# Phase one of a graph network layer: fp32 rows turned once per tile and multiplied in fp32, in place of three bf16 parts

## The chip, the cores and the metric

The kernel runs on one core of a Trainium2 chip. The metric is the device time of one execution in microseconds, the median of the runs given. The engines are TensorE (PE, with its weight loads as PEld), VectorE (DVE), ScalarE (ACT), GpSimd (POOL) and SyncE (SP, which here only issues transfers).

## The reference

Two graph layers over 100,000 nodes of 32 features and 25,000 edges that are sorted by dst. Only the first is touched:

```python
h = maximum(layernorm(x), 0)
x = x + L0(h, src, dst, attr3, attr10, weight)     # phase one
x = x + L1(maximum(layernorm(x), 0), src, dst)     # attention, phase two

# L0: xs = scalars (8) of both ends, xv = vectors (8 x 3) of both ends, 16 each
h = sqrt(2) * relu(emb @ W1 / sqrt(10))                    # (E, 16)
w = (h @ W2 / 4).reshape(E, 7, 16, 8)                      # weights of each edge
s_out = PW_S * (xs . wa_s + (xv . y1) . wb_s / sqrt(3))    # g_out alike
v_out = PW_V * (xs y1 . wc + xv . wd + (xv W3J y2) . we)
out   = segment_sum([tanh(s_out), tanh(g_out) * v_out] * norm, dst)
```

The kernel multiplies each edge's 80 numbers by W2 for each of the 16 hidden units first, and then weights the 16 results by the edge's h and adds them.

## The kernel before

Each of 128 partitions holds T = 196 consecutive edges, and a tile is one edge of each partition. Seven tiles (GA) make a group, and there are NG = 28 groups. GpSimd gathers the rows of x at src and at dst, one indirect transfer for each tile and side, paced by semaphores in `paced(t)`.

Phase one is software-pipelined over the groups, with the order of each engine's instructions written out by hand in a function `group(k, b)` of each engine. For group g+1, VectorE's `normalize` writes `hrow`: for each tile 5 units of 16 fp32 columns (the scalars of both ends, three components of the vectors, and the vectors' product with the edge's direction). ScalarE's `first_parts` and `second_parts` and VectorE's `first_rest` and `third_part` split these into three bf16 parts, stacked as 6 slots of 16 columns for each unit. TensorE's `turn_units` transposes the 35 units of a group in five chunks of seven, through two PSUM banks (turnA, turnB), and ScalarE's `turned` copies each chunk to SBUF.

`product(g, b, t)` multiplies a tile's turned stacks (K = 96) by W2: two matmuls of 384 columns for scalars and gates and three of 128 for the vectors, into one of two buffers of PSUM, `tens`. A product waits until the tile before the last has been read from its buffer. VectorE's `multiply` weights six of the seven tiles by the hidden values (L1408), and ScalarE's `multiply` weights tile 3 in 16 instructions (L809). TensorE then adds the 16 terms with an identity matrix: `sum_first` for tiles 0 to 2 after VectorE's `halve`, `sum_rest` for tiles 3 to 6. VectorE's `outputs` makes `vmix` from these sums, ScalarE's `gates` takes tanh, and VectorE's `messages` scans the running sums.

TensorE's order in a group is: products 0 and 1, `turn_emb`, chunks 2 and 3, `sum_first(g-1)`, chunk 4, product 2, `sum_rest(g-1)`, product 3, the hidden product, products 4 and 5, chunks 0 and 1 of g+1, product 6. ScalarE's is: the first and second parts, `gates(g-1)`, `multiply` (tile 3), squares of g+2, the hidden values, chunks 0 and 1, deviation, chunks 2 to 4 with `keep_run` and `flags` between. Into this are woven the layer norms of all nodes in 28 slices of "dense" rows, some of them beside the edge groups in `SLICE1`:

```python
SLICE1 = {g: d for d, g in enumerate(g for g in range(-1, NG)
          if g not in (2, 5, 8, 11, 14, 16, 17, 20, 22, 24, 25, 27))}
```

With g in SLICE1, VectorE takes row sums and centres in group g, then the variance, and scales and adds in group g+1; each of these five passes is over 124x928 elements.

Before the loop, W2 is loaded, scaled, split into three bf16 parts on VectorE, and copied by 18 transfers of SP's queue (L601, L602) into the stacks `w_s` and `w_v`. Behind phase one come a search for the sums of the source nodes, and phase two, which is of the same shape as phase one, in fp32.

Of the kernel before, what the change touches and what calls it, by code (L numbers as in the profile page):

```python
# [5 lines left out]
F32 = mybir.dt.float32  # L6
# [22 lines left out]
def build_gnn(nc, x, src, dst, attr10, attr3, weight, W1, W2, Wq, Wk, Wv, Wout, out):  # L29
# [8 lines left out]
    SC = 4 * MOUT  # L38
# [18 lines left out]
    assert 0 < TAIL <= T and NG % 2 == 0 and GA % 2 == 1 and NCH % 2 == 1 and T % GA == 0 and 0 < DLAST < DR and DREM <= DP and HEADS == 4  # L57
    assert N <= 4 * 25600 and UNITS * GA == CH * NCH

# [41 lines left out]
    with ctx:  # L101
# [9 lines left out]
        def part(area, at, *dims, parts=P):  # L111
# [4 lines left out]
                if len(dims) > 1 else v  # L116
# [34 lines left out]
        turned_area = sb("stack_turned", [P, UNITS * GA, P], BF16)  # L151
        at = 0
        stack = part(agg, at, SLOTS * NR * ROW // 2).bitcast(BF16).rearrange("p (n s c) -> p n s c", s=SLOTS, c=VU)
        at += SLOTS * NR * ROW // 2
        stackT = [part(agg, at, UNITS * GA * P // 2, parts=KU).bitcast(BF16).rearrange("c (u e) -> c u e", e=P),
                  turned_area[0:KU]]
        at += UNITS * GA * P // 2
# [6 lines left out]
        rest = part(agg, at, UNITS * GA, VU)  # L164
        at += NR * ROW
# [3 lines left out]
        hflat = hrow.rearrange("p t u c -> p (t u) c")  # L169
# [68 lines left out]
        numer = part(turned_area[:, :, :].rearrange("p u e -> p (u e)").bitcast(F32), 0, 2, HEADS * F1, GA + 1)  # L238
# [28 lines left out]
        identb = sb("identb", [P, P], BF16)  # L267
        eps = sb("eps", [P, 1])
        wscale = sb("wscale", [P, 1])
# [52 lines left out]
        w2s = part(h1d_area, at, HID, OG, parts=SC)  # L322
        at += HID * OG
# [6 lines left out]
        w2s_rest = part(h1d_area, at, HID, OG, parts=SC)  # L330
        at += HID * OG
        w2v_rest = part(h1d_area, at, HID, MOUT, parts=VU)
        at += HID * MOUT
        w2s_part = part(h1d_area, at, 3 * HID * OG // 2, parts=SC).bitcast(BF16).rearrange(
            "p (a j o) -> p a j o", a=3, o=OG)
        at += 3 * HID * OG // 2
        w2v_part = part(h1d_area, at, 3 * HID * MOUT // 2, parts=VU).bitcast(BF16).rearrange(
            "p (a j o) -> p a j o", a=3, o=MOUT)
        at += 3 * HID * MOUT // 2
# [42 lines left out]
        s_w2p = sem("w2_parts_ready")  # L382
        s_w2 = sem("w2_stacks_loaded")
# [29 lines left out]
        s_hi = sem("first_parts_ready")  # L413
        s_r1 = sem("first_rests_ready")
        s_mid = sem("second_parts_ready")
        s_lo = sem("stacks_ready")
        s_turn = sem("units_turned")
        s_turned = sem("turned_units_on_sbuf")
# [106 lines left out]
        N_STACKS = 3 * SLOTS  # L525
# [3 lines left out]
        def _(sp):  # L529
# [107 lines left out]
        def _(pool):  # L637
# [6 lines left out]
            pool.wait_ge(s_id, 1)  # L644
            nc.gpsimd.tensor_copy(identb[:], ident[:]).then_inc(s_id, 1)

            def paced(t):

                if t == 10:
                    pool.wait_ge(s_gsb, 1)  # L650
                elif t == 11:
                    pool.wait_ge(s_w2p, 1)
                elif t == 12:
                    pool.wait_ge(s_cen, 1)
                elif t == 13:
                    pool.wait_ge(s_h, 1)
                elif t == 14:
                    pool.wait_ge(s_hi, 1)
                elif t == 15:
                    pool.wait_ge(s_lo, 1)  # L660
                elif 15 < t < 20:
                    pool.wait_ge(s_turned, t - 15)
                elif t >= 20:
                    pool.wait_ge(s_tens, max(t - AHEAD + 1, (3 * (t - 19) + 3) // 4))
# [53 lines left out]
        def _(act):  # L718
# [11 lines left out]
            for rows, plan in ((slice(0, VU), (WA_S, WA_G, WC)), (slice(VU, SC), (WB_S, WB_G, WE))):  # L730
                for col, which in enumerate(plan):
                    load(w2s[rows, :, col * MOUT:(col + 1) * MOUT], w2_rows[which])
# [69 lines left out]

# [28 lines left out]
            first_parts(0)  # L831
            second_parts(0)
# [3 lines left out]
            turned(0, 0, range(2))  # L836
            dense_square(0)
            square(1)
            turned(0, 0, range(2, NCH))
# [3 lines left out]
            def group(k, b):  # L843
# [23 lines left out]
                if next1:  # L867
                    turned(g + 1, 1 - b, range(2, 3))
                if past(g, 0):
                    keep_run(g - 1, 1 - b)  # L870
                if next1:
                    turned(g + 1, 1 - b, range(3, 4))
                flags(g, b)
                if next1:
                    turned(g + 1, 1 - b, range(4, NCH))

# [131 lines left out]
        def _(pe):  # L1008
            pe.wait_ge(s_id, 2)
# [23 lines left out]
            pe.wait_ge(s_feat, 16 * 9)  # L1033
            pe.wait_ge(s_w2, 16 * N_STACKS)

# [13 lines left out]
            def turn_units(n, b, chunks):  # L1049
                pe.wait_ge(s_lo, n + 1)  # L1050
                for c in chunks:
                    if past(n, 0) or c > 1:
                        pe.wait_ge(s_turned, n * NCH + (c - 1))
                    bank = turn[(b + c) % 2][0:KU, :].bitcast(BF16)
                    for i in range(CH):
                        mm = nc.tensor.transpose(bank[:, i * P:(i + 1) * P],  # L1056
                                                 stack[:, c * CH + i].rearrange("p s c -> p (s c)"), identb[:])
                    mm.then_inc(s_turn, 1)

            def product(g, b, t):  # L1060
                pe.wait_ge(s_turned, g * NCH + ((UNITS * t + UNITS - 1) // CH + 1))
# [34 lines left out]
            def group(k, b):  # L1096
# [24 lines left out]
            turn_units(0, 0, range(2))  # L1121
# [120 lines left out]
        def _(dve):  # L1242
# [8 lines left out]
            v.memset(dprev_i, 0).then_inc(s_padf, 1)  # L1251
            v.memset(w1bd[:], 0.0)
# [18 lines left out]
            v.memset(wscale[0:SC], 1.5 ** 0.5 * PW_V)  # L1271
            v.drain()
            v.memset(wscale[0:VU], PW_V)
# [66 lines left out]
            v.tensor_scalar(w2s[:, :, 0:2 * MOUT], w2s[:, :, 0:2 * MOUT], PW_S, None, ALU.mult)  # L1340
            v.tensor_scalar(w2s[:, :, 2 * MOUT:], w2s[:, :, 2 * MOUT:], wscale[0:SC, 0:1], None, ALU.mult)
# [3 lines left out]
            v.drain()  # L1345
            for which in range(3):
                for whole, left, parts in ((w2s, w2s_rest, w2s_part), (w2v, w2v_rest, w2v_part)):
# [525 lines left out]
```

## Time and profile before

| | us |
|---|---|
| median of 3 timed runs (1193.73 to 1196.26) | 1195.46 |
| span of the profiled execution | 1442.6 |
| profiled span over the median | 247.1 |
| PE busy, share of the span | 856.9, 59% |
| DVE busy | 982.3, 68% |
| ACT busy | 842.4, 58% |
| POOL busy | 794.9, 55% |
| mean granted TensorE clock | 0.76 |

The profile is of one execution, whose own time is its span, from the first to the last instruction; what lies around the span is not recorded. Busy time counts an engine's own work; waits do not count. The granted clock is a share of full speed: 1.00 is 2.4 GHz and 0.50 is 1.2 GHz. Phase one lies between about 45 and 785 us of the span, the search between 785 and 1100, and phase two after it. In the chain of waits, each piece is the work or the wait that the next piece had to wait for.

### The profile page before, as it was taken

The page shows a single profiled execution, that of the slowest core. Times are in us where ns is not written, and L with a number is a line of the kernel's source. Part 1 is how long each engine was busy: PE and PEld are TensorE (multiplying, and loading weights), DVE is VectorE, ACT ScalarE, POOL GpSimd, SP SyncE. Part 2 cuts the span into 40 slices and gives each one's busy share as a digit, 9 for nine tenths or more (in the row PEclk, how much of TensorE's full clock was granted, in tenths as well). Part 3 has the DMA queues.
Part 4 walks back from the last instruction along what each step waited for, and adds up shares of the span by engine and source line. Part 5 has one row for each costly group of instructions (what it writes and reads, how often), then busy time and mean ns, then how long its engine had stood idle before and what let it go on. Part 6 is the DMA issues. An engine that isn't in the chain of part 4 may idle for free.

```text
span 1442.6 us, 16871 instructions
## 1 busy us (share of the span) xinstructions
PE 856.9 (59%) x5248; PEld 690.5 (48%) x5248; DVE 982.3 (68%) x1799; ACT 842.4 (58%) x2035; POOL 794.9 (55%) x796
## 2 busy tenths in 40 slices
PE   0256777677776877777874221323135777777773
PEld 0245665566565756666773110211123565555552
DVE  4566686777776667566664635865336999998984
ACT  0346665666766575666754333746244887787871
POOL 5664565466554665455004455775752665656664
PEclk9988688878777777767786555555557999999986
DMA  4121021111111102111014213432300000000000
GB/s 114 19 56 35 16 50 22 43 28 46 58 41 29 37 10 62 34 36 23 16 52 163 76 37 84 115 109 76 88 20 5 10 9 9 9 9 9 9 9 7
DMA packets 40669, 60.52 MB, mean 42 GB/s; under 512 B 17361, under 2 KB 31077, under 8 KB 40324
## 3 DMA queue, kind: packets, MB, share of 16 engines
q1 hardware_dynamic: 12216, 46.86, 10.2%
q0 software_dynamic: 25184, 12.32, 5.4%
q8 instruction: 43, 0.70, 0.2%
q10 hardware_dynamic: 3180, 0.26, 0.2%
q14 instruction: 46, 0.38, 0.1%
HBM read 40.33 MB, written 19.37 MB: 41 GB/s over the span
## 4 chain that ended last, share of the span: by engine, by line
PE 21%; ACT 21%; DVE 20%; another core or an unknown queue 16%; DVEq 10%; issue 8%; SPq 1%; DMA 1%; POOL 0%; POOLq 0%
PE sums L1080 9%; ACT h1d_or_products L809 5%; DVEq L1764 4%; PE tens L1070 3%; ACT below L900 3%; PE turnB L1056 3%; PE turnA L1056 2%; ACT stack_turned L800 2%; DVEq L1705 2%; DVE run L1753 2%; ACT agg_or_stacks L800 2%; DVE tens L1725 2%; PE tens L1074 2%; DVE dcen L1748 1%
## 5 line engine op out<-in xcount | busy, mean ns | idle before, releaser
L674 POOL DMA_INDIRECT x_rows<-in_x,src_index x196 | 196.1, 1001 | 228.9 <-PE tens L1074 146.3
L701 POOL DMA_INDIRECT out_dram<-agg_or_stacks,scatter_index x196 | 193.6, 988 | 144.6 <-ACT agg_or_stacks L974 90.4
L694 POOL DMA_INDIRECT agg_or_stacks<-run_sums,sum_row_index x196 | 203.1, 1036 | 112.3 <-issue 57.9
L674 POOL DMA_INDIRECT x_rows<-in_x,dst_index x196 | 197.2, 1006 | 64.9 <-issue 64.9
L1408 DVE TENSOR_TENSOR h1d_or_products<-tens,hid 128x768 f32<-128x768 f32 x168 | 158.8, 952 | 64.8 <-PE tens L1074 42.8
L1080 PE MATMUL sums<-h1d_or_products,ident 128*128 128x192 f32 x896 | 174.4, 356 | 4.8 <-issue 4.2
L1080 PEld LDWEIGHTS sums<-h1d_or_products,ident 128*128 128x128 f32 x896 | 164.9, 212 | 11.3 <-issue 11.1
L1143 PE MATMUL sums<-one_column,halves_or_steps 128*128 128x1 f16 x112 | 22.1, 197 | 176.6 <-DVE halves_or_steps L1564 62.0
L967 ACT ACTIVATE features_or_rows<-stack_turned,is_last 128x132 f32<-128x132 f32 x196 | 85.9, 520 | 39.3 <-DVE stack_turned L1735 39.3
L1143 PEld LDWEIGHTS sums<-one_column,halves_or_steps 128*128 128x128 f16 x112 | 14.1, 126 | 197.7 <-ACT below L900 73.2
L1070 PE MATMUL tens<-w_scalar_stacks,agg_or_stacks 96*128 96x384 bf16 x196 | 66.5, 432 | 65.9 <-ACT h1d_or_products L809 41.4
L1070 PE MATMUL tens<-w_scalar_stacks,stack_turned 96*128 96x384 bf16 x196 | 66.6, 433 | 62.2 <-ACT h1d_or_products L809 48.8
L900 ACT ACTIVATE below<-sums,bias_of_src 128x196 bf16<-128x196 f32 x112 | 46.5, 420 | 83.6 <-remote 55.2
L800 ACT COPY stack_turned<-turnB 96x896 bf16<-96x896 bf16 x42 | 37.9, 902 | 97.1 <-remote 68.4
L809 ACT ACTIVATE h1d_or_products<-tens,hid 128x48 f32<-128x48 f32 x448 | 88.8, 358 | 0.1
L1080 PE MATMUL sums<-halves_or_steps,ident 128*128 128x144 f32 x448 | 83.1, 351 | 3.4 <-issue 3.1
L1391 DVE TENSOR_TENSOR agg_or_stacks<-agg_or_stacks 128x560 f32<-128x560 f32 x28 | 20.8, 741 | 91.0 <-ACT agg_or_stacks L791 91.0
L800 ACT COPY agg_or_stacks<-turnA 96x896 bf16<-96x896 bf16 x42 | 38.0, 904 | 73.3 <-remote 47.5
L1080 PEld LDWEIGHTS sums<-halves_or_steps,ident 128*128 128x128 f32 x448 | 78.6, 250 | 3.2 <-issue 3.2
L1212 PE MATMUL turnB<-features_or_rows,ident 128*128 128x132 f32 x448 | 60.2, 290 | 31.1 <-ACT features_or_rows L967 24.5
L1056 PE MATMUL turnB<-identb,agg_or_stacks 128*96 128x128 bf16 x490 | 59.9, 289 | 24.0 <-ACT stack_turned L800 20.6
L1212 PEld LDWEIGHTS turnB<-features_or_rows,ident 128*128 128x128 f32 x448 | 55.3, 197 | 38.1 <-ACT features_or_rows L967 30.1
(308 smaller groups left out, 2536.5 us busy)
## 6 DMA issues: line engine op xcount, KB each, us to landing
src_everywhere<-src_by_columns SPq DMA_DIRECT2D x14, 896.0 KB
xin<-in_x SPq DMA_DIRECT2D x27, 449.5 KB
out_dram<-xin SPq DMA_DIRECT2D x27, 449.5 KB
x_rows<-in_x,src_index POOLq DMA_INDIRECT x196
x_rows<-in_x,dst_index POOLq DMA_INDIRECT x196
run<-run_sums SPq DMA_DIRECT2D x1, 3136.0 KB
agg_or_stacks<-run_sums,sum_row_index POOLq DMA_INDIRECT x196
out_dram<-agg_or_stacks,scatter_index POOLq DMA_INDIRECT x196
```

Source lines behind the costliest of these rows:

```text
L674: nc.gpsimd.indirect_dma_start(xs[:, t, side, :], None, x, bass.IndirectOffsetOnAxis(ap=idx[:, t:t + 1], axis=0)).then_inc(s_gath[g % LEAD ...
L694: nc.gpsimd.indirect_dma_start(aggr[:, t, :], None, rs, bass.IndirectOffsetOnAxis(ap=ridx[:, t:t + 1], axis=0)).then_inc(s_rsg[t // GA], 16)
L701: nc.gpsimd.indirect_dma_start(out, bass.IndirectOffsetOnAxis(ap=sidx[:, t:t + 1], axis=0), aggr[:, t, :], None, bounds_check=N - 1, oob_i ...
L800: nc.scalar.copy(stackT[b][:, c * CH:(c + 1) * CH, :].rearrange("c u e -> c (u e)"), turn[(b + c) % 2][0:KU, :].bitcast(BF16)[:, 0:CH * P] ...
L809: last = nc.scalar.activation(prod[:, 2 * TACT:2 * TACT + 2, j, :], bank[:, :, j * OG:(j + 1) * OG], ACT.Copy, scale=hid[:, b, TACT, j:j + 1])
L900: last = nc.scalar.activation(below[:, t % 4], bank[:, j * T:(j + 1) * T], ACT.Sigmoid, bias=of[:, t:t + 1], scale=256.0, accum_out=to[:, ...
L967: last = nc.scalar.activation(head_rows[:, t, :], numer[:, b, :, 1 + t], ACT.Copy, scale=last_of_first[:, g * GA + t:g * GA + t + 1])
L1056: mm = nc.tensor.transpose(bank[:, i * P:(i + 1) * P], stack[:, c * CH + i].rearrange("p s c -> p (s c)"), identb[:])
L1070: nc.tensor.matmul(bank[:, 0:HID * OG], stackT[b][:, UNITS * t + u, :], w_s[:, i].rearrange("c j o -> c (j o)"), start=(i == 0), stop=(i = ...
L1080: mm = nc.tensor.matmul(sums[:, a * OUTS:b * OUTS].rearrange("p (c o) -> p c o", o=OG), ident[:], terms[:, :, j, :], start=(j == 0), stop= ...
L1212: nc.tensor.matmul(head_sum, ident[:], head_rows[:, t, :], start=(t == 0), stop=(t == GA))
L1408: v.tensor_tensor(prod[:, 2 * t:2 * t + 2], tens[(b + t) % 2][:, :].rearrange("p (a c) -> p a c", a=2)[:, :, 0:HID * OG].rearrange("p a (j ...
```

## The change

The split into bf16 parts goes. `turn_units` turns each tile's 80 fp32 columns of `hrow` at once, in two halves of 4 and 3 tiles (`TURNS`), a whole group ahead, and ScalarE copies the two halves (512 and 384 columns of 80 partitions). A product is two fp32 matmuls with K = 80 and 384 columns each; `w_v` has its columns laid out so that one matmul serves the three components, with zeros where a unit has no weight. The buffers of both turned groups lie in `turned_area`. W2 stays fp32, and 3 transfers in place of 18 copy it. `normalize` waits until the rows before it have been turned. `paced` waits on other semaphores for tiles 14 to 19.

```diff
-    SLOTS = 6
     UNITS = 5
-    KU = SLOTS * VU
+    KU = UNITS * VU
-    CH = 7
-    NCH = UNITS * GA // CH
+    TURNS = ((0, 4), (4, GA))
...
-        w_s = sb("w2_scalar_stacks", [KU, 2, HID, OG], BF16)
-        w_v = sb("w2_vector_stack", [KU, HID, MOUT], BF16)
+        w_s = sb("w2_of_scalars", [KU, HID, OG])
+        w_v = sb("w2_of_vectors", [KU, HID, OG])
...
-            for place, which in enumerate((0, 0, 1, 1, 2, 0)):
-                rows = slice(place * VU, (place + 1) * VU)
-                for u in range(2):
-                    sp.dma_start(w_s[rows, u, :, :], w2s_part[u * VU:(u + 1) * VU, which]).then_inc(s_w2, 16)
-                sp.dma_start(w_v[rows, :, :], w2v_part[:, which]).then_inc(s_w2, 16)
+            for k in range(3):
+                sp.dma_start(w_v[(k + 1) * VU:(k + 2) * VU, :, k * MOUT:(k + 1) * MOUT], w2v).then_inc(s_w2, 16)
...
# ScalarE
-            def first_parts(n):
-                act.wait_ge(s_h, n + 1)
-                nc.scalar.copy(stack[:, :, 0:SLOTS:2, :], spread(hflat, 2, [P, UNITS * GA, 3, VU])).then_inc(s_hi, 1)
-
-            def second_parts(n):
-                act.wait_ge(s_r1, n + 1)
-                nc.scalar.copy(stack[:, :, 1:4:2, :], spread(rest, 2, [P, UNITS * GA, 2, VU])).then_inc(s_mid, 1)
-
-            def turned(n, b, chunks):
-                for c in chunks:
-                    act.wait_ge(s_turn, n * NCH + (c + 1))
-                    nc.scalar.copy(stackT[b][:, c * CH:(c + 1) * CH, :].rearrange("c u e -> c (u e)"),
-                                   turn[(b + c) % 2][0:KU, :].bitcast(BF16)[:, 0:CH * P]).then_inc(s_turned, 1)
+            def turned(n, b, half):
+                of = slice(TURNS[half][0] * P, TURNS[half][1] * P)
+                act.wait_ge(s_turn, n * 2 + (half + 1))
+                nc.scalar.copy(stackT[b][:, of], turn[half][0:KU, 0:of.stop - of.start]).then_inc(s_turned, 1)
...
# ScalarE, group(k, b)
                 if next1:
-                    first_parts(g + 1)
                     take_emb(g + 1)
-                    second_parts(g + 1)
...
                 if next1:
                     hidden(g + 1, 1 - b)
-                    turned(g + 1, 1 - b, range(2))
+                    turned(g + 1, 1 - b, 0)
...
                 flags(g, b)
                 if next1:
-                    turned(g + 1, 1 - b, range(4, NCH))
+                    turned(g + 1, 1 - b, 1)
...
# TensorE
+            def turn_units(n, half):
+                pe.wait_ge(s_h, n + 1)
+                if past(n, 0):
+                    pe.wait_ge(s_turned, n * 2 - 1 + half)
+                first, end = TURNS[half]
+                for t in range(first, end):
+                    mm = nc.tensor.transpose(turn[half][0:KU, (t - first) * P:(t - first + 1) * P],
+                                             hrow[:, t].rearrange("p u c -> p (u c)"), ident[:])
+                mm.then_inc(s_turn, 1)
...
             def product(g, b, t):
...
-                for i, u in enumerate((0, UNITS - 1)):
-                    nc.tensor.matmul(bank[:, 0:HID * OG], stackT[b][:, UNITS * t + u, :],
-                                     w_s[:, i].rearrange("c j o -> c (j o)"), start=(i == 0), stop=(i == 1))
-                vec = bank[:, 512:512 + HID * OG].rearrange("p (j o) -> p j o", o=OG)
-                for k in range(3):
-                    mm = nc.tensor.matmul(vec[:, :, k * MOUT:(k + 1) * MOUT], stackT[b][:, UNITS * t + 1 + k, :], w_v[:],
-                                          start=True, stop=True)
-                mm.then_inc(s_tens, 1)
+                rows = stackT[b][:, t * P:(t + 1) * P]
+                nc.tensor.matmul(bank[:, 0:HID * OG], rows, w_s[:].rearrange("c j o -> c (j o)"), start=True, stop=True)
+                nc.tensor.matmul(bank[:, 512:512 + HID * OG], rows, w_v[:].rearrange("c j o -> c (j o)"), start=True,
+                                 stop=True).then_inc(s_tens, 1)
...
# TensorE, group(k, b)
                 if more:
                     turn_emb(g + 1)
-                turn_units(g, b, range(2, 4))
                 if past(g, 0):
                     sum_first(g - 1)
-                turn_units(g, b, range(4, NCH))
                 product(g, b, 2)
...
                 product(g, b, 4)
+                if more:
+                    turn_units(g + 1, 0)
                 product(g, b, 5)
                 if more:
-                    turn_units(g + 1, 1 - b, range(2))
+                    turn_units(g + 1, 1)
                 product(g, b, 6)
...
# VectorE
+            v.memset(w_s[:], 0.0)
+            v.memset(w_v[:], 0.0)
...
             def normalize(n):
                 dve.wait_ge(s_std, n + 1)
+                if past(n, 0):
+                    dve.wait_ge(s_turn, n * 2)
...
-            def first_rest(n):
-                dve.wait_ge(s_hi, n + 1)
-                v.tensor_tensor(rest, hflat, stack[:, :, 0, :], ALU.subtract).then_inc(s_r1, 1)
-
-            def third_part(n):
-                dve.wait_ge(s_mid, n + 1)
-                v.tensor_tensor(stack[:, :, SLOTS - 1, :], rest, stack[:, :, 1, :], ALU.subtract).then_inc(s_lo, 1)
```

On VectorE the calls of `first_rest` and `third_part` in `group` go too, and the three rounds of casts and subtractions of W2.

## Rows read from the trace of the kernel before

**Rows 1.** The page: the span, and the chain's shares by engine.

```profile
span 1442.6 us, 16871 instructions
...
PE 21%; ACT 21%; DVE 20%; another core or an unknown queue 16%; DVEq 10%; issue 8%; SPq 1%; DMA 1%; POOL 0%; POOLq 0%
```

**Rows 2.** The chain's shares by line, 84 to 780 us.

```profile
by line: PE sums L1080 17.9%; another core or an unknown queue 17.2%; ACT h1d_or_products L809 10.7%; PE tens L1070 7.1%; issue 6.2%; PE turnB L1056 5.1%; PE turnA L1056 4.5%; ACT stack_turned L800 4.5%; ACT agg_or_stacks L800 3.6%; PE tens
```

**Rows 3.** Timeline (start, duration, engine, line, operation [idle before, releaser]).

```profile
418.34 0.95 PE L1056 MATMUL turnA<-identb,agg_or_stacks 128*96 128x128 bf16 x7
...
426.13 0.90 ACT L800 COPY agg_or_stacks<-turnA 96x896 bf16<-96x896 bf16 x1 [8.06 <-remote]
```

**Rows 4.** The chain in order of time (start, duration, what), late in phase one.

```profile
699.98 5.27 PE sums L1080 x32
...
706.31 3.18 ACT h1d_or_products L809 x16
...
709.62 0.80 PE tens L1070 x2
...
717.16 2.73 PE sums L1080 x16
...
720.77 5.27 PE sums L1080 x32
...
741.12 5.27 PE sums L1080 x32
```

**Rows 5.** The chain in order of time, the first 104 us.

```profile
34.58 0.35 DVE h1d_or_products L1348
...
38.00 0.60 SPq L601
...
102.26 1.97 PE sums L1080 x5
```

**Rows 6.** Stretches: length; busy PE, PEld, DVE, ACT, POOL; clock, DMA share, GB/s.

```profile
709.60:718.50 8.90, 8.69 (x55) 7.09 (x56) 7.29 (x13) 6.31 (x10) 0.00 (x0) 0.50 0.01 2
718.60:727.00 8.40, 8.40 (x65) 7.94 (x64) 4.82 (x9) 5.36 (x8) 0.00 (x0) 1.00 0.00 0
727.00:747.35 20.35, 16.29 (x122) 14.02 (x120) 13.09 (x20) 12.35 (x30) 0.00 (x0) 0.83 0.08 22
386.00:409.05 23.05, 17.52 (x119) 14.78 (x120) 19.68 (x31) 16.46 (x37) 12.66 (x14) 0.78 0.14 29
1231.00:1295.00 64.00, 47.45 (x258) 37.71 (x257) 58.73 (x119) 50.93 (x120) 38.45 (x40) 1.00 0.04 9
```

**Rows 7.** Timeline of TensorE in phase two.

```profile
1249.42 1.13 PE L1183 MATMUL tens<-gbd,features_or_rows 128*128 128x512 f32 x2 [1.49 <-ACT features_or_rows L947]
1250.38 0.81 PE L1185 MATMUL tens<-gbd,features_or_rows 96*128 96x384 f32 x2
1251.05 0.70 PE L1199 MATMUL tens<-ubd,features_or_rows 128*128 128x256 f32 x2
...
1259.11 0.27 PE L1177 MATMUL turnA<-ident,h1d_or_products 128*96 128x128 f32 x1
1259.22 0.27 PE L1176 MATMUL turnA<-ident,agg_or_stacks 128*128 128x128 f32 x1
```

**Rows 8.** Groups by line and shape (count | busy us, mean ns | idle before).

```profile
L791 ACT CAST agg_or_stacks<-agg_or_stacks 128x1680 bf16<-128x1680 f32 x28 | 44.7, 1595 | 4.8 <-DVE agg_or_stacks L1387 4.8
...
L795 ACT CAST agg_or_stacks<-agg_or_stacks 128x1120 bf16<-128x1120 f32 x28 | 31.5, 1127 | 26.3 <-DVE agg_or_stacks L1391 23.6 <-issue 2.6
...
L800 ACT COPY agg_or_stacks<-turnB 96x896 bf16<-96x896 bf16 x28 | 25.3, 902 | 19.5 <-remote 12.9 <-PE turnA L1056 4.5 <-PE turnB L1056 1.8
...
L1391 DVE TENSOR_TENSOR agg_or_stacks<-agg_or_stacks 128x560 f32<-128x560 f32 x28 | 20.8, 741 | 91.0 <-ACT agg_or_stacks L791 91.0
```

**Rows 9.** The chain in order of time, 386 to 409 us.

```profile
398.44 2.87 another core or an unknown queue
```

**Rows 10.** Timeline of VectorE: group 2's row sums.

```profile
70.76 0.62 DVE L1359 TENSOR_REDUCE stat<-x_rows 128x14 f32<-128x448 f32 x1 [4.26 <-DMA x_rows<-in_x,dst_index]
```

More of the change, by code:

```diff
@@ L56, in build_gnn @@
     DREM = N - DP * RPP
-    assert 0 < TAIL <= T and NG % 2 == 0 and GA % 2 == 1 and NCH % 2 == 1 and T % GA == 0 and 0 < DLAST < DR and DREM <= DP and HEADS == 4
-    assert N <= 4 * 25600 and UNITS * GA == CH * NCH
+    assert 0 < TAIL <= T and NG % 2 == 0 and GA % 2 == 1 and T % GA == 0 and 0 < DLAST < DR and DREM <= DP and HEADS == 4
+    assert N <= 4 * 25600 and all((b - a) * P <= 512 for a, b in TURNS)
     HALF = T // 2
@@ L148, in build_gnn @@
         h1d = part(h1d_area, 0, T, FEAT)
-        turned_area = sb("stack_turned", [P, UNITS * GA, P], BF16)
+        turned_area = sb("stack_turned", [P, 2 * HEADS * F1 * (GA + 1)])
+        assert 2 * GA * P <= 2 * HEADS * F1 * (GA + 1)
+        stackT = [part(turned_area, b * GA * P, GA * P, parts=KU) for b in range(2)]
         at = 0
[L153 to L157, printed above, removed]
         cen = part(agg, at, NR, FEAT)
@@ L237, in build_gnn @@
         assert at <= T * FEAT
-        numer = part(turned_area[:, :, :].rearrange("p u e -> p (u e)").bitcast(F32), 0, 2, HEADS * F1, GA + 1)
+        numer = part(turned_area, 0, 2, HEADS * F1, GA + 1)
         late = sb("halves_or_steps", [P, CT * P // 2 + 4 * T])
@@ L412, in build_gnn @@
         s_h = sem("normalized_rows_ready")
[L413 to L418, printed above, removed]
+        s_turn = sem("stacks_turned")
+        s_turned = sem("turned_stacks_on_sbuf")
         s_tens = sem("tensor_product_ready")
@@ L657, in paced @@
                 elif t == 14:
-                    pool.wait_ge(s_hi, 1)
+                    pool.wait_ge(s_turn, 1)
                 elif t == 15:
-                    pool.wait_ge(s_lo, 1)
-                elif 15 < t < 20:
-                    pool.wait_ge(s_turned, t - 15)
+                    pool.wait_ge(s_turn, 2)
+                elif t == 16:
+                    pool.wait_ge(s_turned, 1)
+                elif t == 17:
+                    pool.wait_ge(s_turned, 2)
+                elif t == 18:
+                    pool.wait_ge(s_hid, 1)
+                elif t == 19:
+                    pool.wait_ge(s_tens, 1)
                 elif t >= 20:
@@ L729, in _ @@
             load(w2e, w2_rows[WE])
-            for rows, plan in ((slice(0, VU), (WA_S, WA_G, WC)), (slice(VU, SC), (WB_S, WB_G, WE))):
+            for rows, plan in ((slice(0, VU), (WA_S, WA_G, WC)), (slice(KU - VU, KU), (WB_S, WB_G, WE))):
                 for col, which in enumerate(plan):
-                    load(w2s[rows, :, col * MOUT:(col + 1) * MOUT], w2_rows[which])
+                    load(w_s[rows, :, col * MOUT:(col + 1) * MOUT], w2_rows[which])
             for t in range(GA):
@@ L835, in _ @@
             hidden(0, 0)
-            turned(0, 0, range(2))
+            turned(0, 0, 0)
+            turned(0, 0, 1)
             dense_square(0)
             square(1)
-            turned(0, 0, range(2, NCH))
             deviation(1)
@@ L1047, in hidden_product @@
                 nc.tensor.matmul(small[:, P:P + GA * HID], embT[:], w1bd[:], start=True, stop=True).then_inc(s_hps, 1)
[L1049 to L1058, printed above, removed]
+            def turn_units(n, half):
[7 more added lines that the diff above has]
+                mm.then_inc(s_turn, 1)
             def product(g, b, t):
-                pe.wait_ge(s_turned, g * NCH + ((UNITS * t + UNITS - 1) // CH + 1))
+                pe.wait_ge(s_turned, g * 2 + (1 if t < TURNS[0][1] else 2))
                 if past(g, 0) or t > 1:
@@ L1120, in _ @@
             hidden_product(0)
-            turn_units(0, 0, range(2))
+            turn_units(0, 0)
+            turn_units(0, 1)
             group(0, 0)
@@ L1339, in _ @@
             dve.wait_ge(s_wl, 16 * N_LOADS)
-            v.tensor_scalar(w2s[:, :, 0:2 * MOUT], w2s[:, :, 0:2 * MOUT], PW_S, None, ALU.mult)
-            v.tensor_scalar(w2s[:, :, 2 * MOUT:], w2s[:, :, 2 * MOUT:], wscale[0:SC, 0:1], None, ALU.mult)
+            for rows, gain in ((slice(0, VU), PW_V), (slice(KU - VU, KU), 1.5 ** 0.5 * PW_V)):
+                v.tensor_scalar(w_s[rows, :, 0:2 * MOUT], w_s[rows, :, 0:2 * MOUT], PW_S, None, ALU.mult)
+                v.tensor_scalar(w_s[rows, :, 2 * MOUT:], w_s[rows, :, 2 * MOUT:], gain, None, ALU.mult)
             v.tensor_scalar(w2d, w2d, PW_V * 3.0 ** -0.5, None, ALU.mult)
@@ L1344, in _ @@
             v.scalar_tensor_tensor(w2v, w2e, -PW_V * 6.0 ** -0.5, w2d, ALU.mult, ALU.add)
-            v.drain()
-            for which in range(3):
-                for whole, left, parts in ((w2s, w2s_rest, w2s_part), (w2v, w2v_rest, w2v_part)):
-                    v.tensor_copy(parts[:, which], whole if which == 0 else left)
-                v.drain()
-                for whole, left, parts in ((w2s, w2s_rest, w2s_part), (w2v, w2v_rest, w2v_part)):
-                    if which < 2:
-                        v.tensor_tensor(left, whole if which == 0 else left, parts[:, which], ALU.subtract)
-                v.drain()
             v.drain().then_inc(s_w2p, 1)
@@ L1465, in _ @@
             normalize(0)
-            first_rest(0)
-            third_part(0)
             dense_sums(0)
@@ L1524, in group @@
                     dense_sums(SLICE1[g])
-                if next1:
-                    first_rest(g + 1)
                 if g in SLICE1:
@@ L1533, in group @@
                 halve(g)
-                if next1:
-                    third_part(g + 1)
                 if past(g, 0):
```

38 lines of the change are left out of this document (5 added, 33 removed).

## The prediction

> **What bounds the kernel now.** I read the page first. Its span is 1442.6 us, 247.1 more than the median of the timed runs, 1195.46, and 16% of its chain, some 236 us, stands under "another core or an unknown queue" on a kernel of one core [rows 1]. The chain of the edge phase alone says where: 17.2% of 696 us, 120 us [rows 2]. The timeline shows what such a piece is. Seven turns into turnA end at 419.3 by TensorE's records, and ScalarE's copy of that bank starts at 426.13 after 8.06 us of idle time put down to "remote" [rows 3]. In the last three groups, when GpSimd has no gathers left, there is no such piece. I take it that these pieces belong to the profiled execution: 1442.6 - 236 = 1206 is within 1% of the median. So I price a group on the undisturbed ones near 700 to 747 us, apply the difference to the median, and predict nothing about the span.
>
> The chain there is one loop [rows 4]. sum_rest (32 records, 5.27 us) runs to 705.25. VectorE then builds vmix, ScalarE takes the gates and works off tile 3 in 16 instructions of 3.18 us together, and TensorE's product 5, whose PSUM buffer tile 3 held, starts at 709.62: a hand-over of 4.37 us. From there the chain is on TensorE until the next sum_rest at 720.77, 11.15 us: product 5, two banks of turns, products 6, 0 and 1, turn_emb, two more banks, sum_first, the fifth bank, product 2. The loop takes 20.79 us; the next one 20.35. Against it: from the first sum_rest at 102.26 [rows 5] to 741.12 lie 26 intervals, 638.9 us; less the 120 us that is 20.0 each.
>
> The stretches [rows 6] add the clock. From 709.6 to 718.5, behind a wait of 3.1 us, TensorE is granted half speed (1.2 GHz) while it is 98% busy; from 718.6 full speed (2.4 GHz). So 8.9 us of the 11.15 run at half. VectorE is busy for 13.1 us in the light group from 727 and for 19.7 in a group with dense rows on both sides (386.0 to 409.05). By SLICE1 six of the 27 are such "double" groups; ten ("single") carry a dense variance ahead of multiply 6 and a scale and add behind it; eleven are "light": two have no dense rows, nine only row sums and a centre, which fit under sum_rest.
>
> **The change, part by part.**
>
> *Products.* Five bf16 matmuls of 1,152 columns become two fp32 matmuls of 384. An fp32 matmul of 96 rows by 384 columns shows as two records, and from its first to the next line's first is 0.67 us at full clock [rows 7]. K=80 for 96 is no reason for another price. So a product takes 1.33 us at full clock and 2.6 at half. Before, at half, product 5 took 0.80 for its first two matmuls, 1.12 with the other three [rows 4].
>
> *Turns.* Thirty-five bf16 turns become seven fp32 turns. Those that follow one another in phase two start 0.11 us apart [rows 7]; at half I take 0.21. Four (0.44) lie before product 5, in the wait for ScalarE, where they cost nothing as long as products 3 and 4 leave 0.44 of it; three lie between products 5 and 6.
>
> *The loop, light group, full clock.* sum_rest 5.27; hand-over 4.37, nothing in it changed. Then five products 6.65, three turns 0.33, turn_emb 0.11, and sum_first 16 records at 144/192 of sum_rest's 0.165, 1.98: 9.07 instead of 11.15. Together 18.7, 2.1 less than 20.8. That needs the full clock between 709.6 and 718.5, and this is my choice in the sum. During the hand-over TensorE now has product 3, the hidden product (0.2), product 4 and four turns: 1.33 + 0.2 + 1.33 + 0.44 = 3.3, which leaves an idle 1.1 in place of 3.1. In phase two TensorE is 74% busy, with waits of 1.49 us before L1183, and is granted 1.00 over 64 us [rows 6, 7]. The new loop would be 94% busy (17.6 of 18.7) with a shorter wait. The Trainium skill (TensorE: Matmul & The Clock Gate, Part 4) says that turns do not count as activity for the clock. By that rule the quiet piece is 1.5 us, the length that phase two bears, so the sum would stay; the trace neither contradicts nor shows the rule.
>
> *Dense rows.* In a single group ScalarE's square and VectorE's variance sum come ahead of multiply 6, and product 1 waits for that: about 0.75 us more in the new loop, a part of which the old one pays too. I take a gain of 1.3. In double groups VectorE decides. It loses 0.74 for first_rest, as much for third_part of the same shape, and its wait for ScalarE's cast, 91.0 us in all and 3.3 per group [rows 8], nearly the whole of the 3.4 that it idles in that group. So it is busy 18.2 us; with 0.9 for drains and gaps and about 2 of waits for the longer products 5, 6 and 1 (an estimate), it gets round in 21. The old double group, 23.05 less an unknown piece of 2.87 [rows 9], takes 20.2. I take a loss of 1.0, for what the piece hid.
>
> *ScalarE.* It loses 1.60 + 1.13 + 5 x 0.90 = 7.2 us per group and gains two copies of 512 and 384 fp32 columns, some 1.1 by the copy of 896 [rows 8]. None of it is on the loop: tile 3 is released by the gates, and the copy that product 0 waits for stands behind ScalarE's squares, where one of 0.6 replaces two of 0.9. Hidden behind products 5 and 6 (2.7 us), so I take nothing; if this cover went, it would cost its 0.6. normalize's new wait, for the turns of the rows that it overwrites, is met before the group begins: nothing.
>
> *Clock in double groups.* There TensorE idles near 3 us (VectorE is late by 2, ScalarE by 1), the length that costs it the clock now [rows 6]. Busy time at half costs half its length: 4.4 for a stretch like today's 8.9, less for a shorter one. I take 2.6, and charge three of six: 8 us. Bounds: 0 and 6 x 4.4 = 26.
>
> *Start.* SP has 3 weight copies to issue for 18, at 0.60 each, and VectorE none of the splits, which fill the 3.4 us from 34.58 to 38.00 [rows 5]; two memsets of 384 columns are new (under 1). TensorE starts some 10 us earlier, but group 2's last gather, for which VectorE waited 4.26 us [rows 10], is issued by GpSimd at 2.5 us a tile. Bounds of the gain 0 and 12; I take 5, near the row of the wait.
>
> *Sum.* 11 x -2.1 - 10 x 1.3 + 6 x 1.0 = -30; clock +8; start -5: -27 from 1195.46, so 1169 us (1168.5). Phase two, the search and the last gathers are untouched. GpSimd needs 17.5 us for 14 gathers (1.0 and a gap of 0.25 each), under 18.7.
>
> **Rivals.**
> - *The clock stays half behind the hand-over* (the other side). Place: products 5, 6, 0, 1. Each microsecond at half costs 0.5. If 8.9 us per group stay at half as now, the light loop is 18.7 + 4.45 = 23.2, 2.4 over the old one: 27 x 2.4 - 5, 1255. With 3.4 us of it in each of 24 groups: 1169 + 24 x 1.7 = 1210. It turns the sign when more than 2 us per group run at half. For it: fp32 work has more to lose. Against it: the 64 us above. Chance 0.20.
> - *VectorE becomes the bound everywhere.* Multiplies 5, 6, 0 and 1 wait for products of 1.5 us with their way to PSUM, while the dense passes pile up behind. Light groups would gain 0.5 to 1, single ones nothing, double ones lose 1.5: 1185 to 1197. For it: 19.7 busy of 23. Against it: light groups with 13.1. Chance 0.17.
> - *More is gained*: the timed group is the 20.8 of the late groups throughout, double ones included (21.5), and no clock is lost. Then double groups lose nothing, single ones gain 1.7: 11 x 2.1 + 17 + 5 = 45, so 1150; with 10 of start 1145. Chance 0.15.
> - *My forecast*: 1158 to 1183. Chance 0.48.
>
> **Range and chances.** 1169, with 1142 to 1212 for 8 in 10: it takes in the third rival, the second and the short drops of the first. This kernel's runs differ by about 0.2%, 2.4 us. Faster by more: my case, the third rival and a third of the second, 0.68; within 0.2%: 0.07; slower: 0.25.
>
> **What would show it.** In undisturbed groups, sum_rest to sum_rest 18.7 to 19.5, granted clock 1.00 in between, product 5's first two matmuls 1.3 us for four records, a wait before it near 1.1. In double groups VectorE's idle time near 3 us and period 21. The copies of the turned stacks at 0.5 to 0.6 us, two per group. Wrong if the granted clock behind the hand-over is 0.5, if VectorE waits for TensorE in light groups, or if the early groups, which the profile disturbs, go otherwise in the timed runs.

## The result and the profile after

The changed kernel takes 1282.52 us (1280.81 to 1294.43, four runs) where the kernel before takes 1195.62 on the same chip: 1.0758 times as long, with a 95% interval of 1.071 to 1.0806. It is slower by some 87 us. The forecast was 1169 with a range of 1142 to 1212, so the sign and the range both missed.

The page of the changed kernel, to be read against [rows 1]. Its own time is 1280.85 us beside a span of 1279.1.

```profile
span 1279.1 us, 14681 instructions
...
PE 948.2 (74%) x4268; PEld 682.9 (53%) x4268; DVE 941.4 (74%) x1735; ACT 675.5 (53%) x1895; POOL 806.8 (63%) x795
...
PEclk9998977787877878979878655555579999999986
...
PE 40%; ACT 20%; DVE 17%; DVEq 9%; DMA 6%; issue 4%; POOL 3%; SPq 0%; POOLq 0%
PE sums L1033 15%; PE tens L1027 11%; PE tens L1028 11%; ACT h1d_or_products L774 7%; ACT features_or_rows L924 6%; DVEq L1697 4%; POOL x_rows L648 3%; DMA out_dram<-xin 3%; DMA xin<-in_x 3%; ACT L913 3%; DVE run L1686 2%; DVE tens L1658 2%; ACT run L915 2%; ACT below L857 1%; PE turnB L1013 1%
```

There is no "another core or unknown queue" in this chain. TensorE heads it, and the granted clock is 7 or 8 tenths in most slices of phase one. Its chain in order of time, one group from hand-over to hand-over (start, duration, what), against [rows 4]. It is a single group; the light one before it, from 397.2 to 421.2 by its gates, takes the same 24.0, for both have their whole chain on TensorE and ScalarE's tile 3:

```profile
420.94 0.66 PE tens L1028 x2
421.60 0.02 issue
421.62 3.17 ACT h1d_or_products L774 x16
424.80 0.14 issue
424.93 0.88 PE tens L1027 x2
425.81 0.88 PE tens L1028 x2
426.70 0.64 PE turnB L1013 x3
427.34 1.28 PE tens L1027 x2
428.62 1.28 PE tens L1028 x2
...
435.02 0.21 PE small L998
435.23 2.56 PE sums L1033 x16
437.79 0.65 PE tens L1027 x2
438.44 0.65 PE tens L1028 x2
439.08 5.20 PE sums L1033 x32
444.29 0.65 PE tens L1027 x2
...
445.59 0.02 issue
```

From one "issue" behind product 3 to the next it is 23.99 us. All of TensorE's work between 426 and 436 takes twice what the same lines take outside: a matmul of 384 columns 1.28 for 0.65, turn_emb 0.21 for 0.11. The stretches of this kernel say why (columns as in [rows 6]):

```profile
402.20:412.40 10.20, 10.20 (x24) 6.10 (x23) 4.76 (x8) 4.02 (x9) 7.63 (x9) 0.50 0.25 60
412.40:426.00 13.60, 12.21 (x65) 9.92 (x65) 10.35 (x19) 5.12 (x21) 6.36 (x6) 1.00 0.06 7
```

For 10.2 us TensorE is busy without a gap and is granted half speed (1.2 GHz); then comes full speed (2.4 GHz). By the starts of the gates' instruction, once per group, 17 of the 27 intervals are 23.7 to 25.8 us, with a granted clock of 0.73 to 0.79. Nine, in which the clock does not fall, are 19.0 to 21.3, and the last one, behind the last group, is 19.5 with a clock of 0.74. The first gate starts at 92.9 and the last at 708.5: 22.8 us per group.

### The profile page after: what moved, and what is told of

The parts are those of the page before. It is cut to its first block, busy times and chain, and to the rows that moved or that the text cites. A ratio compares the mean times of both kernels' runs of the same rounds, so it can differ in the third digit from the quotient of the medians.

```text
span 1279.1 us, 14681 instructions
## 1 busy us (share of the span) xinstructions
PE 948.2 (74%) x4268; PEld 682.9 (53%) x4268; DVE 941.4 (74%) x1735; ACT 675.5 (53%) x1895; POOL 806.8 (63%) x795
## 4 chain that ended last, share of the span: by engine, by line
PE 40%; ACT 20%; DVE 17%; DVEq 9%; DMA 6%; issue 4%; POOL 3%; SPq 0%; POOLq 0%
PE sums L1033 15%; PE tens L1027 11%; PE tens L1028 11%; ACT h1d_or_products L774 7%; ACT features_or_rows L924 6%; DVEq L1697 4%; POOL x_rows L648 3%; DMA out_dram<-xin 3%; DMA xin<-in_x 3%; ACT L913 3%; DVE run L1686 2%; DVE tens L1658 2%; ACT run L915 2%; ACT below L857 1%; PE turnB L1013 1%
## 5 line engine op out<-in xcount | busy, mean ns | idle before, releaser
L648 POOL DMA_INDIRECT x_rows<-in_x,src_index x196 | 208.2, 1062 | 158.8 <-PE tens L1028 113.6
L1027 PE MATMUL tens<-w_of_scalars,stack_turned 80*128 80x384 f32 x392 | 207.1, 617 | 61.4 <-ACT h1d_or_products L774 40.4
L1028 PE MATMUL tens<-w_of_vectors,stack_turned 80*128 80x384 f32 x392 | 206.1, 615 | 0.0
L1033 PEld LDWEIGHTS sums<-h1d_or_products,ident 128*128 128x128 f32 x896 | 147.6, 191 | 7.2
L1033 PE MATMUL sums<-h1d_or_products,ident 128*128 128x192 f32 x896 | 150.6, 327 | 0.0
L786 ACT ACTIVATE gate<-sums 128x112 f32<-128x112 f32 x28 | 7.4, 263 | 246.8 <-DVE vmix L1421 246.8
L1027 PEld LDWEIGHTS tens<-w_of_scalars,stack_turned 80*128 80x128 f32 x392 | 81.9, 237 | 101.0 <-issue 97.5
L1028 PEld LDWEIGHTS tens<-w_of_vectors,stack_turned 80*128 80x128 f32 x392 | 94.0, 240 | 74.7 <-issue 40.3
L1668 DVE TENSOR_TENSOR_SCAN stack_turned<-run,tens 128x1024 f32<-128x1024 f32 x28 | 63.3, 2261 | 0.2 <-issue 0.2
L754 ACT COPY embT<-small 70x128 f32<-70x128 f32 x28 | 7.3, 261 | 99.5 <-PE small L998 99.5
```

The lines of the kernel that those rows point to most:

```text
L648: nc.gpsimd.indirect_dma_start(xs[:, t, side, :], None, x, bass.IndirectOffsetOnAxis(ap=idx[:, t:t + 1], axis=0)).then_inc(s_gath[g % LEAD ...
L1027: nc.tensor.matmul(bank[:, 0:HID * OG], rows, w_s[:].rearrange("c j o -> c (j o)"), start=True, stop=True)
L1028: nc.tensor.matmul(bank[:, 512:512 + HID * OG], rows, w_v[:].rearrange("c j o -> c (j o)"), start=True, stop=True).then_inc(s_tens, 1)
L1033: mm = nc.tensor.matmul(sums[:, a * OUTS:b * OUTS].rearrange("p (c o) -> p c o", o=OG), ident[:], terms[:, :, j, :], start=(j == 0), stop= ...
L1668: v.tensor_tensor_scan(numer[:, b, 0:HF].rearrange("p n t -> p (n t)"), decay[:, b, 0:HF].rearrange("p n t -> p (n t)"), terms.rearrange(" ...
```

## Experiments

The changed kernel has two places where its clock could be helped: the rows that its matmuls fill (80), and the wait before product 5. Each comparison below is with the kernel before on the same chip.

**e1_k128, e2_k96: the products filled up to 128 or 96 rows.** The spare rows of the turned stacks hold zeros, and so do those of the weights, so that the sums are unchanged.

```diff
+        KP = 128                                   # e2: 96
-        stackT = [part(turned_area, b * GA * P, GA * P, parts=KU) for b in range(2)]
+        stackT = [part(turned_area, b * GA * P, GA * P, parts=KP) for b in range(2)]
-        w_s = sb("w2_of_scalars", [KU, HID, OG])
+        w_s = sb("w2_of_scalars", [KP, HID, OG])   # w_v likewise
-                nc.scalar.copy(stackT[b][:, of], turn[half][0:KU, 0:of.stop - of.start]).then_inc(s_turned, 1)
+                nc.scalar.copy(stackT[b][0:KU, of], turn[half][0:KU, 0:of.stop - of.start]).then_inc(s_turned, 1)
+            v.memset(turned_area[0:KP, 0:2 * GA * P], 0.0)
```

> The changed kernel with the contraction padded from 80 to 128 rows: rows 80 to 127 of the turned stacks and of both weight tiles are zero. Columns and instructions of TensorE are the same. Theory A (the chip weighs the rows that a matmul fills, so that products of 80 rows do not bring the clock back and products of 128 would): the half-speed stretches of 10.2 us behind each wait shrink to about 3.4, most groups fall from 24.0 towards 19.0 to 20.7 us, and the time from 1282 to 1180-1225. Theory B (only whether TensorE works counts, and the idle 1.4 us per group is what costs the clock): nothing changes, 1275 to 1290.

> As the kernel with 128 rows, but padded to 96 only, the K of the kernel before. Theory A with rows weighed one by one: between the two, 1240 to 1280. Theory A with rows weighed in blocks of 32: 80 rows fill three blocks already, so no change, 1275 to 1290. Theory B: no change.

**e3_fill6: 80 rows, with the wait before product 5 filled.** Six fp32 matmuls of the identity by itself go into spare columns of turnB; no one reads them.

```diff
+                pe.wait_ge(s_turned, 2 * (g + 1))
+                for _ in range(6):
+                    nc.tensor.matmul(turn[1][:, 3 * P:], ident[:], ident[:], start=True, stop=True)
                 # product 5
```

> The changed kernel with six extra fp32 matmuls of the identity by itself (128 columns, 0.22 us each at full clock, 1.3 us together) into an unused corner of turnB's bank, placed in TensorE's wait before product 5. They compute nothing that is used. Theory B: the wait of 1.4 us is filled, the clock stays at full speed in every light group, periods of 19.0 to 19.6 and a time of 1170 to 1200. Theory A: the same here, since a full clock is then never lost; it differs only if a drop happens at the start or in double groups, from which it would not recover before sum_first: 1180 to 1220. If neither holds and the price of the fp32 products is itself higher than the 1.3 us of the full clock, the time stays above 1260.

**e0_before_again: the kernel before, unchanged,** beside them.

> The kernel before, unchanged, for a second profile. If the pieces put down to an unknown queue belong to the profiled execution, its timed runs stay at 1195 and the profile has them again, perhaps in other places; group periods without them should be near 19.6, which is what the timed runs leave for a group when the rest of the changed kernel's span (667 us outside the 27 intervals) is taken off.

Measured, on a chip where the kernel before takes 1422.98 us (1406.67 to 1437.72, 13 runs): e1 1342.04, ratio 0.943 (0.9359 to 0.95); e2 1354.95, 0.9511 (0.9453 to 0.957); e3 1360.56, 0.955 (0.9499 to 0.9602); e0 1421.6, 1.0019 (0.997 to 1.0068). No expectation was laid on a chip like this. What it did tell is about my baseline: e0's profiled execution has a span of 1413.4 and a time of its own of 1415.15, and its timeline has the piece of [rows 3]:

```profile
573.05 0.95 PE L1056 MATMUL turnB<-identb,agg_or_stacks 128*96 128x128 bf16 x7
...
580.90 0.90 ACT L800 COPY stack_turned<-turnB 96x896 bf16<-96x896 bf16 x1 [8.33 <-remote]
```

The turns end at 574.0 by their records and the copy starts 6.9 us later. This execution took no longer than the others of its run (1415 to 1436), so these pieces are in timed runs too. They go with that chip, or with its state at the time, and not with profiling.

**f0_after, f1_k128_again, f4_fill6_again, f5_before_profile: the same on an ordinary chip,** with the changed kernel and the kernel before unchanged.

> The changed kernel itself, so that it stands beside the others on one chip. In the last comparison the kernel before took 1423 us, and its first median was 1196: something outside the program costs it 227 us there. Theory C (the cost is paid when TensorE's completions reach the others late while gathers run, and it is paid on some chips and not on others): where before takes 1420, the changed kernel takes 1370 to 1400, the sign of the change turned; where before takes 1196 it takes 1282. Theory D (the 1282 was itself a run with the cost in it): it takes 1282 on both.

> The changed kernel with K padded to 128 by zero rows, again, beside the changed kernel itself. Theory A (rows count for the clock): where before takes 1196, near 1185, and 40 to 100 us under the changed kernel anywhere. Theory B (only being busy counts): no difference from the changed kernel beyond 5 us.

> The changed kernel with six identity matmuls in the wait before product 5, again. Theory B: as fast as with K of 128 or faster, 1170 to 1200 where before takes 1196. Theory A: the clock is lost less often, but in double groups it still is, and then it is half for 10 us: between the changed kernel and the padded one, 20 to 80 us under the changed kernel.

> The kernel before once more. If this comparison runs where it takes 1196, its profile should have no pieces put down to an unknown queue and a period near 19.6; if it takes 1420, it looks as in the other two profiles, and the quiet one stays unseen.

Measured, with the kernel before at 1190.65 (1187.29 to 1200.15, 25 runs): f0 1278.59, 1.0721 (1.0661 to 1.0781); f1 1192.16, 1.0013 (0.9989 to 1.0037); f4 1187.54, 0.9968 (0.9945 to 0.9992); f5 1192.32, 0.9999. Either edit alone takes back the whole loss: 86.4 us by the rows, 91.1 by the filled wait. The wait itself may stay as it is. The timelines of TensorE ahead of product 5, the changed kernel first:

```profile
422.94 0.60 PE L1013 MATMUL turnA<-ident,agg_or_stacks 128*80 128x128 f32 x4
424.93 0.88 PE L1027 MATMUL tens<-w_of_scalars,stack_turned 80*128 80x384 f32 x2 [1.39 <-ACT h1d_or_products L774]
```

Then f1, with 128 rows:

```profile
412.19 0.60 PE L1014 MATMUL turnA<-ident,agg_or_stacks 128*80 128x128 f32 x4
414.19 0.88 PE L1028 MATMUL tens<-w_of_scalars,stack_turned 128*128 128x384 f32 x2 [1.40 <-ACT h1d_or_products L775]
```

The turns before the wait and the wait are equal (1.39 and 1.40 us); only the rows differ. Behind it, in f1's chain:

```profile
414.19 0.88 PE tens L1028 x2
415.07 0.65 PE tens L1029 x2
...
416.05 0.65 PE tens L1028 x2
```

The products stay at 0.65 where those of the changed kernel go to 1.28. f4's chain has the wait filled (L1069), and its products stay at 0.65 with 80 rows:

```profile
410.69 1.34 PE turnB L1069 x12
412.03 0.05 issue
412.09 0.88 PE tens L1027 x2
412.97 0.65 PE tens L1028 x2
...
413.95 0.65 PE tens L1027 x2
```

Six fillers take 1.34 us, 0.22 each. Product 5 starts 0.14 us after ScalarE's tile 3 has ended (at 411.95), as it does in the changed kernel, so they put nothing on the loop. The 540 us from 100 to 640 in one row each: the changed kernel of f0, then f1, f4, and the kernel before of f5.

```profile
100.00:640.00 540.00, 506.18 (x1983) 365.73 (x1983) 373.44 (x614) 231.71 (x696) 339.44 (x323) 0.81 0.16 38
```

```profile
100.00:640.00 540.00, 479.64 (x2329) 359.53 (x2329) 422.00 (x706) 266.71 (x809) 341.38 (x328) 0.97 0.19 47
```

```profile
100.00:640.00 540.00, 511.45 (x2654) 394.39 (x2655) 423.70 (x708) 269.02 (x819) 342.13 (x330) 0.98 0.19 49
```

```profile
100.00:640.00 540.00, 431.08 (x3206) 377.40 (x3206) 448.71 (x752) 414.31 (x932) 329.63 (x325) 0.83 0.18 45
```

The clock goes from 0.81 to 0.97 and 0.98, VectorE gets more done in the same time (373 to 422 busy), and TensorE in f1 is even less busy than in f0. ScalarE's relief, 414 to 232 busy, bought nothing.

**g1_before_fill, g2_before_fill12: the kernel before with its wait filled,** by 26 or by 12 fp32 matmuls of 64 columns.

```diff
+                pe.wait_ge(s_turned, (g + 1) * NCH)
+                for i in range(12):                # g1: 26
+                    nc.tensor.matmul(turn[i % 2][:, 448:512], ident[:], ident[:, 0:64], start=True, stop=True)
                 # product 5
```

> The kernel before with 26 small identity matmuls (fp32, 64 columns, 2.8 us together at full clock) into a free corner of the two turn banks, in TensorE's wait of 3.1 us before product 5. They compute nothing that is used. If the half clock behind the wait costs the kernel before too, as its groups of 17.6 us (clock 1.00) beside those of 19.8 say, light groups come to 17.6 to 18, double groups stay at VectorE's 20 to 21, and the time falls to 1150-1175 where before takes 1191. If that clock was hidden by other work in the kernel before, 1185 to 1195.

> The kernel before with 12 filling matmuls of 64 columns in the wait before product 5 in place of 26. The 26 took 5.8 us (0.22 us each, not the 0.11 that their columns alone would take) in a wait of 3.1, and put 2.7 us on the loop; 12 take 2.7 us. If the half clock costs the kernel before, light groups come to 17.6 and the time to 1150-1175 where before takes 1190. If not, 1185 to 1195.

g1: 1240.33 us against 1189.54, 1.0409 (1.0371 to 1.0446). Twenty-six fillers of 0.22 are 5.8 us in a wait of some 3: they came to stand on the loop, a miss of my sizing. g2, with 2.7 us of them: 1170.42 (1166.09 to 1171.59) against 1192.8, 0.9811 (0.9784 to 0.9838). That beats both kernels. So the kernel before also paid for the clock, 22 us. In the quiet profile of f5 its light groups go both ways: four of eleven are at 1.00 and take 17.57, six at 0.83 and take 19.8 to 19.9. The first row is one of the four, the second one of the six:

```profile
294.50:312.10 17.60, 13.56 (x123) 12.11 (x121) 16.14 (x27) 15.33 (x35) 13.49 (x14) 1.00 0.38 119
353.00:372.90 19.90, 16.58 (x124) 14.54 (x122) 16.26 (x28) 15.34 (x35) 13.56 (x15) 0.83 0.21 49
```

In g2 ten of the eleven light groups are at 1.00, seven of them at 17.6 us, and the chain there lies on GpSimd, whose gathers set that pace: 14 per group at 1.25 us from start to start.

```profile
413.13 0.95 POOL x_rows L674
414.08 0.30 issue
414.38 0.94 POOL x_rows L674
```

**f2_k128_fill, f3_k128_ones, f6_k96_again, f7_k88: what about the rows counts?** f2 has both edits; f3 is f1 with ones in the spare rows of the turned stacks (times zero weights); f7 fills up to 88 rows.

```diff
+            v.memset(turned_area[0:KP, 0:2 * GA * P], 1.0)    # f3, KP = 128
+        KP = 88                                               # f7
```

> The changed kernel with both cures: K of 128 and the six filling matmuls. If both act on the same thing, the granted clock, the time is that of the filled kernel (1187 where before takes 1191), at most 3 us less. If one of them has an effect of its own, the two gains add: below 1175.

> As the kernel with K of 128, but the 48 spare rows of the turned stacks hold ones where they held zeros; the weights under them stay zero. If the chip counts rows that take part, whatever they hold, the same time as with zeros (1192 where before takes 1191), within 3 us. If what the rows hold counts, the clock returns sooner and the few groups of 20.4 to 20.6 us go to 19.6: 5 to 8 us less.

> The changed kernel with K padded to 96. Where before takes 1191 and the changed kernel 1279: rows counted one by one, 1200 to 1265, since the drop is shorter or rarer; rows counted in blocks of 32 (80 rows fill three already), 1270 to 1285; a threshold between 80 and 96, 1190 to 1200 as with 128.

> The changed kernel with K padded to 88. At 80 rows the clock drops in most groups (1279 where before takes 1190), at 96 in almost none (1194). If the chip weighs single rows against a level, some groups drop: anything between 1194 and 1279, most likely 1200 to 1260. If it counts whole blocks of 32 rows that are full, 1270 to 1285.

Measured against 1189.54 (21 runs): f2 1189.45, 0.9998 (0.9985 to 1.001); f3 1193.12, 1.0035 (1.002 to 1.0049); f6 1194.41, 1.0032 (1.0006 to 1.0057). The two edits don't add up, as two ways to the same thing wouldn't. What the spare rows hold makes no difference that the runs show (f1 1192.16, f3 1193.12, on two chips). f7, against 1192.8, took 1213 to 1214.6 in three runs with a mean granted clock of 0.87, and 1192.58 in a fourth with 0.89. So 88 rows do as 96 in one execution and cost some 20 us in the others. In the profiled one (1213.18) four groups take 25.3 to 25.4 us at 0.73, where the others hold 1.00. Its chain in one of the four:

```profile
222.72 1.28 PE tens L1028 x2
224.00 1.28 PE tens L1029 x2
...
230.40 0.21 PE small L999
230.62 3.73 PE sums L1034 x16
234.34 0.65 PE tens L1028 x2
```

With 80 rows the clock is lost in most groups, with 88 in four in the profiled execution, with 96 and 128 for a short piece in three or four (0.85 to 0.92). 80, 88 and 96 rows all fill three blocks of 32, so it isn't the number of blocks.

**h2_after_again: the changed kernel on f7's chip.**

> The changed kernel once more. On a chip where before takes 1190: 1276 to 1285. On one where before takes 1420, which is what this run is for: between 1360 and 1400, so that the change is faster there and slower here. Its cause would be the number of TensorE's instructions, which the change lowers from 242 to 172 per group, if late completions come once per so many of them.

It took 1284.74 (1276.63 to 1295.93), 1.0754 (1.0712 to 1.0796): the loss is not one of a chip.

## Why the prediction was wrong

- **The step that failed: "That needs the full clock between 709.6 and 718.5, and this is my choice in the sum."** I chose it because the wait shrinks to 1.1 us, and phase two bears 1.49 at full clock [rows 7]. The wait did shrink, to 1.4, and the clock fell behind it all the same. What I compared with were matmuls of 96 and 128 rows. With 80, the same 1.4 us cost the clock in most groups (the changed kernel beside f1), and TensorE, then busy without a gap, stayed at half for 10.2 us. At half a product takes 2.56, as priced, so that a light group takes 24.0 for 19.03. f4 less the changed kernel puts the whole at 91 us; over the 27 intervals between gates, 22.80 less 19.50 us each is 89. That is the larger part of the 114 us between forecast and result; the other 24 are the gain that isn't there at full clock either (f4, 1187.54 against 1190.65, gains 3 of the 27), and the next points say why.
- **The rival that came true** is the first, clock at half behind the hand-over. Its light loop was 23.2 (24.0 measured), its price 0.5 per us at half holds (10.2 x 0.5 = 5.1 for the 4.97 between the two kinds of group), and 1210 to 1255 was still short: I let the clock be lost for 8.9 us as now. Fully busy at half, TensorE got the clock back later, not sooner: after 10.2 us, where f5's light groups that lose it (0.83 of 19.9 us) are at half for some 6.8. The chance of 0.20 was too low. Against it stood only rows of a stretch with other shapes.
- **The baseline was the second error.** "I take it that these pieces belong to the profiled execution" is wrong: e0 shows them in an execution of 1415 us. The profile, 1442.6 us, fits a chip where this kernel takes over 1400, and the median of 1195 one like f5's; which chips they were is not on record. On f5's a group is not 20.8 but, by the gates of f5 (90.2 and 623.8), 19.76 on average, with light groups of 17.57 where the clock holds. So my loop gain of 2.1 was measured from a group that had lost the clock (0.75 from gate to gate), and credited the change with the return of it.
- **At equal clock the change is slower.** With the clock at 1.00 from gate to gate, light groups take 19.03 against 17.57. Single ones take 19.6 to 19.8 (f4) against 19.0 to 19.5 (three of g2), leaving out the last of each, and double ones 21.3 against 20.2 (one of g2). In f5 no single or double group keeps the full clock; they take 19.3 to 21.3 at 0.75 to 0.92. Filled against filled, the kernels take 1187.54 and 1170.42, from different chips with the kernel before at 1190.65 and 1192.8. The five products cost 6.5 us for 2.5 (0.33 and 0.17 for the two kinds of matmul in f5's chain), and the turns saved (35 x 0.055 = 1.9, for 7 x 0.11 = 0.8) don't pay for it.
- **The hand-over, 4.37 "nothing in it changed",** measured 4.64 (from sum_rest's end at 444.29 back one group: 0.65 + 0.66 + 0.02 + 3.17 + 0.14). I had missed that product 3, now 1.31, comes ahead of ScalarE's work and is longer than VectorE's vmix. With it the loop is 19.0 where I had 18.7.
- **The start, "I take 5",** measured nothing. The first gate stands at 92.9, in f5 at 90.2. In both kernels the chain of the start is GpSimd's gathers at 1.25 us each, up to 57.8 and 58.2, then their DMA, and VectorE's row sum starts at 60.25 after and 60.57 before. The splits that went away had been hidden by them. My lower bound of the gain, 0, was nearest. From there the changed kernel runs its first products at half clock, 2.56 each; that these make the 2.7 was not tested.
- **Right:** the price of a product at either clock (1.30 and 2.56; I had 1.33 and 2.6), turns of 0.11 and 0.21, single groups of 19.5 (19.56 in f4) and double ones of 21 (21.29) where the clock holds, GpSimd under the loop, and no worth in ScalarE's relief. Light, single and double groups at full clock came out within 0.35 us; the timed kernel mostly did not run at it.
- **The 8 us for the clock in double groups** were put in the wrong place. Where the clock is kept at all (f1, f4) every interval of a double group is at 1.00. f1 loses it for a short piece in four single groups right behind a double one (0.92 from gate to gate), 0.8 to 1.0 us each, under 4 us in all.
- The rule of the Trainium skill that I weighed (TensorE: Matmul & The Clock Gate, Part 4: turns don't count as activity) can't be the cause by itself. f1 has the same turns before the same wait and keeps the clock. The same page of the Trainium skill says ("Why this matters for your kernels") that one matmul of few rows takes as long as one of 128. The traces agree as to the duration (0.65 us at 80, 96 and 128 rows with the clock full). For what rows do to the clock, only these runs speak.

Some things stay open. The changed kernel itself was not timed on a chip like that of e0. There its padded and filled forms were 4.5 to 5.7% faster than the kernel before. Their matmuls are fewer (4268 and 4604 for 5248), and "another core or an unknown queue" has 4.5 and 4.7% of the chain from 60 to 700 us in e1 and e3, for 10.4 in e0; but that the one explains the other was only argued. On that chip the filled wait is no full remedy either: e3 is at 0.73 to 0.79 in six of 27 intervals. And why nine of the 27 intervals of the changed kernel keep the clock was not settled. They are not always the same ones: seven in f0, and nine in h2 that are partly others.

## What to carry to other kernels

When bf16 matmuls are exchanged for fp32 ones with fewer rows, ask of each wait on TensorE whether the clock will survive it, and compare with a wait between matmuls of as many rows; rows up to 96 or 128 filled with zeros cost no time here and were worth 86 us. A wait that costs the clock can be filled with matmuls that no one reads, sized below the wait: 1.3 us of them gave 91 us, 2.7 us in the kernel before 22, and 5.8 us lost 51. And price a group only from a profile whose own time agrees with the timed median; a gap of 20% between them went here with another chip and other costs, and was not noise to be subtracted.

## What was not expected of the hardware

- The rows of a matmul weigh in the granted clock: 1279 to 1285 us at 80 rows, 1213 (one run of 1193) at 88, 1194 at 96, 1192 at 128, on chips where the kernel before takes 1190 to 1193. Zeros and ones in the spare rows do the same (1192.2, 1193.1).
- TensorE stayed at 0.50 for 10.2 us while it was busy for 10.20 of them, first on matmuls of 80 rows and turns, at the end on sum_first's 128 rows.
- An fp32 matmul of 64 columns took 0.22 us, the same as one of 128 columns (fillers of g1 and f4).
- The same kernel takes 1191 us on one chip and 1423 on another, where ScalarE began 6.9 us after the records that it waited for had ended.
